# A smaller lead of the score maxima in an attention kernel, and the output projection's first pieces moved

## The reference, cut to what matters

```
# x: [2, 1024, 512], 32 heads of 16, all float32
x = x + layernorm(attention(layernorm(x)))          # stage A to C
x = x + layernorm(feed_forward(layernorm(x)))       # stage D: 512 -> 1376 -> 512, silu(gate) * up

# attention
q, k, v = split(x @ w_attn.T); q, k = rope(q), rope(k)
scores  = q @ k.T / sqrt(16), causal                # 1024 x 1024 for each of 64 heads
y       = softmax(scores) @ v
y       = y + gating * softmax(q @ ak.T / sqrt(512)) @ av      # 10 adapter rows
out     = y @ w_proj.T
```

## Time and profile before

| | before |
|---|---|
| three runs | 1182.92, 1190.9, 1196.09 us, median 1190.9 |
| the profiled execution | 1182.43 us, of which the span from first to last instruction is 1180.7 us |
| PE busy | 1095.5 us, 93% of the span |
| DVE, ACT, POOL busy | 703.0, 500.9, 255.1 us |
| mean granted clock of PE | 0.962 of full |
| attention | from about 230 us to 746 us of the span |

### The profile page before, as it was taken

The page is one execution under the profiler, slowest core; times in us unless marked ns, Lnnn a source line. Parts: engine busy times, 40 slices in busy tenths (PEclk is TensorE's granted clock), DMA queues, the critical chain, the costliest instruction groups (busy, mean ns, idle before and its releaser), DMA issues. The chain is left out here.

```text
span 1180.7 us, 18091 instructions
## 1 busy us (share of the span) xinstructions
PE 1095.5 (93%) x7020; PEld 750.4 (64%) x7020; DVE 703.0 (60%) x975; ACT 500.9 (42%) x1054; POOL 255.1 (22%) x255
## 2 busy tenths in 40 slices
PE   3999999888999999999999998889999999999996
PEld 1878778644454555555545444577887887887884
DVE  4748565776777778888888763583634324324113
ACT  3233242334776777777777655224321121121110
POOL 3517255400221111111111133451001001001001
PEclk9999999856999999999999998999999999999998
DMA  6265767733444444445444332645323003001000
GB/s 252 75 178 152 164 177 170 157 78 54 83 84 83 83 84 83 87 94 96 88 84 96 125 104 89 202 160 161 107 58 107 1 1 107 1 1 59 13 1 36
DMA packets 93869, 113.08 MB, mean 96 GB/s; under 512 B 26456, under 2 KB 54744, under 8 KB 93784
## 3 DMA queue, kind: packets, MB, share of 16 engines
q1 hardware_dynamic: 91720, 108.07, 35.9%
q10 hardware_dynamic: 2064, 3.85, 2.0%
HBM read 68.82 MB, written 42.21 MB: 94 GB/s over the span
## 5 line engine op out<-in xcount | busy, mean ns | idle before, releaser
L841 ACT ACTIVATE prob<-ps_s 128x512 f32<-128x512 f32 (+3 forms) x768 | 323.7, 497 | 173.9 <-PE ps_s L991 167.3
L865 DVE TENSOR_REDUCE neg<-ps_m 128x2 f32<-128x1024 f32 (+2 forms) x224 | 248.2, 1144 | 60.4 <-PE ps_m L956 38.3
L991 PE MATMUL ps_s<-q_op,k_op 50*128 50x512 f32 (+2 forms) x768 | 242.3, 448 | 18.4 <-ACT prob L841 13.5
L956 PE MATMUL ps_m<-k_op,q_op 48*128 48x512 f32 (+2 forms) x768 | 186.2, 422 | 9.9 <-DVE neg L865 7.1
L991 PEld LDWEIGHTS ps_s<-q_op,k_op 50*128 50x128 f32 x768 | 117.5, 192 | 120.2 <-ACT prob L841 61.8
L799 POOL TENSOR_SCALAR_AFFINE_SELECT prob<-prob 128x512 f32<-128x512 f32 x128 | 83.3, 651 | 396.7 <-ACT prob L841 396.6
L1005 PE MATMUL ps_y<-prob,vg 128*17 128x512 f32 (+3 forms) x1536 | 152.5, 517 | 0.0
L1577 DVE TENSOR_TENSOR hf<-sl,ps_u 128x512 f32<-128x512 f32 (+1 forms) x44 | 30.2, 686 | 171.5 <-PE ps_u L78 150.8
L865 DVE TENSOR_REDUCE neg_far<-ps_m 128x4 f32<-128x512 f32 (+2 forms) x96 | 100.2, 1048 | 31.1 <-PE ps_m L961 29.5
L956 PEld LDWEIGHTS ps_m<-k_op,q_op 48*128 48x128 f32 x768 | 97.4, 199 | 29.7 <-DVE neg L865 20.4
L1642 PE MATMUL ps_d<-w_high,wp_high 128*128 128x512 f32 (+1 forms) x352 | 115.2, 390 | 0.3 <-DVE wp_high L1579 0.3
(11 more groups left out here) (175 smaller groups left out, 1689.1 us busy)
## 6 DMA issues: line engine op xcount, KB each, us to landing
y_heads<-y_sb SPq DMA_DIRECT2D x32, 256.0 KB, 2.1
raw<-in_w_ffn SPq DMA_DIRECT2D x31, 256.0 KB, 3.3
k_op<-k_parts SPq DMA_DIRECT2D x28, 256.0 KB, 4.4
q_op<-q_parts SPq DMA_DIRECT2D x56, 128.0 KB, 5.0
v_groups<-v_out SPq DMA_DIRECT2D x16, 272.0 KB, 4.1
x<-in_x SPq DMA_DIRECT2D x4, 1024.0 KB, 7.8
q_parts<-part_h SPq DMA_DIRECT2D x16, 256.0 KB, 2.9
q_parts<-part_l SPq DMA_DIRECT2D x16, 256.0 KB, 2.9
```

The source lines that it names most:

```text
L841: act.activation(prob[:, v % NPROB, h, unit_cols(u)], ps_s[:, y % NS, unit_cols(u)], ACT.Exp, scale=D ** -0.5).then_inc(s_exp, 1)
L865: nc.vector.tensor_reduce(to[:, :, pairs[0]:pairs[-1] + 1, i - TT * c], scores, axis=AX.X, op=ALU.max, negate=True).then_inc(a_read, 1)
L956: last = nc.tensor.matmul(ps_m[:, g % 2, s, base:base + wide], q_op[buf][r, c, pair, (i - TT * c) * P:(i - TT * c + 1) * P], k_op[buf][r, ...
L991: nc.tensor.matmul(ps_s[:, y % NS, lo:BLK], k_op[buf][r, pair, j * P:(j + 1) * P], q_op[buf][r, c, pair, lo:BLK], start=True, stop=True)\
```

## The change

LEAD falls from 11 to 3. Group 0 now holds 36 M steps instead of 45 (eight chunks and one turn less), every later group still 22, but other chunks stand in the slots of the pattern, and the list of maxima runs out nine slots later, in the tenth unit of group 14. The slots of `beside` move with it: the four parts of the first projected piece now all stand in group 15, together with those of the second piece. What POOL, ACT and DVE do for these pieces moves to later places.

```
-LEAD = 11
+LEAD = 3
@@ POOL, behind the mask of unit u of group n
-                if (n, u) == (NG - 2, 3):
+                if (n, u) == (NG - 2, 10):
                     tail.add_adapter(pool, 0)
-                if (n, u) == (NG - 2, 9):
+                if (n, u) == (NG - 1, 1):
                     tail.add_adapter(pool, 1)
-                if (n, u) == (NG - 2, 11):
-                    tail.add_adapter(pool, 2)
-                if (n, u) == (NG - 1, 2):
+                if (n, u) == (NG - 1, 3):
                     tail.inverse_deviation(pool, 0)
                     tail.residual_pool(pool, 0)
-                if (n, u) == (NG - 1, 3):
+                    tail.add_adapter(pool, 2)
                     tail.inverse_deviation(pool, 1)
                     tail.residual_pool(pool, 1)
@@ ACT
-        highs = {(NG - 2, 9): 0, (NG - 2, 11): 1, (NG - 1, 2): 2, (NG - 1, 11): 3}
+        highs = {(NG - 1, 0): 0, (NG - 1, 3): 1, (NG - 1, 7): 2, (NG - 1, 11): 3}
@@ DVE, behind the last maxima
         weights(NG - 4, range(2))
+        tail.low(dve, 0)
         tail.divide(dve, 1)
         weights(NG - 4, range(2, 4))
-        tail.low(dve, 0)
+        tail.low(dve, 1)
+        weights(NG - 3, range(4, 5))
+        finish(0)
         tail.divide(dve, 2)
-        weights(NG - 3, range(4, 6))
-        tail.low(dve, 1)
-        finish(0)
+        weights(NG - 3, range(5, 6))
+        finish(1)
         tail.low(dve, 2)
-        finish(1)
         tail.divide(dve, 3)
@@ PE, which work stands in which slot behind the list of maxima
-        (tail.spread, 1, (5, 6)), (tail.spread, 2, (9, 10)),
-        (tail.project, 0, (11, 12, 14, 16)), (tail.project, 1, (19, 21, 23, 25)),
-        (tail.spread, 3, (28, 30))
+        (tail.spread, 1, (5, 6)), (tail.project, 0, (7, 8, 9, 10)),
+        (tail.spread, 2, (11, 12)), (tail.project, 1, (14, 15, 16, 17)),
+        (tail.spread, 3, (19, 20))
```

More of the change, by code:

```diff
@@ L1037, in _ @@
         beside = {}
-        for step, m, slots in ((first_spread, 0, (1, 2)), (last_turn, 0, (3,)), (tail.spread, 1, (5, 6)), (tail.spread, 2, (9, 10)),
-                               (tail.project, 0, (11, 12, 14, 16)), (tail.project, 1, (19, 21, 23, 25)),
-                               (tail.spread, 3, (28, 30))):
+        for step, m, slots in ((first_spread, 0, (1, 2)), (last_turn, 0, (3,)), (tail.spread, 1, (5, 6)),
+                               (tail.project, 0, (7, 8, 9, 10)), (tail.spread, 2, (11, 12)),
+                               (tail.project, 1, (14, 15, 16, 17)), (tail.spread, 3, (19, 20))):
             beside.update((slot, (step, m, part)) for part, slot in enumerate(slots))
```

## The result

The changed kernel takes 1242.7 us (median of 4 runs, 1236.4 to 1250.3) where the kernel before takes 1190.7: a ratio of 1.046, 95% interval 1.042 to 1.050. It is slower by 52 us, and the forecast of 1196 with its range up to 1212 was wrong. The profiled execution took 1243.97 us, its span is 1242.3 us, and its mean granted clock is 0.905 where it was 0.962.

The account below looks back on a forecast made before the run. It took PE and ACT to pace alternating stretches of each group, PE around the products and ACT among the scores. Terms -6 - 2.5 + 11.7 + 2 = +5.2 us on the median 1190.9 gave 1196 us, range 1183 to 1212.

Parts of the forecast that it names:

- Part 1, group 0: Group 0 of attention: nine M steps leave it, saving 6 us, plus 2.5 us from a clock dip that should go.
- the second term: Behind group 0's end: the half-clock dip from 289.4 to 296.2 should go, -2.5 us, from 0 to -3.4.
- Part 2, the steady groups: Groups 1 to 13: same work in other slots, 0.9 us longer each, +11.7 us in all, from +5 to +16.
- the wait: Group's end: PE waits 0.5 us ahead of turn 1 for DVE's read of k1, where it waited for nothing before.
- Part 3, the tail: End of attention: eight chunks and a turn come back in group 14, +2 us, from -1 to +6.
- The two waits: End of attention: first projection's wait for DVE's low and second's for normalize stay unchanged, 2.8 us in all.
- POOL's cover: End of attention: last products may wait for masks behind POOL's earlier work; one or two us, not in the sum.
- SP at no cost: SP's queue: stores and loads go out about 6 us later, maxima still land with 3 us of room; cost 0.
- Rival C: Steady groups: the new 0.5 us wait at the turn drops the clock in each group, +21 us, 1217 us; chance 0.09.
- against: a group would still be busy near 95%: Steady groups: the prediction's argument that PE, still busy near 95%, speaks against the clock falling in each group.

Follow-up runs that it names:

- no_masks: Kernel before, with the causal masks of chunks k14 and k15 left out in groups 1 to 14: 1215.0 us, ratio 1.021.
- single: Changed kernel with the products in twelve single blocks, one behind each second score pair, M steps where they were: 1191.2 us, ratio 1.003.
- far_late: Changed kernel with the second half's far-key chunks first and turn 1 moved from behind score pair 22 to behind 24: 1239.0 us, ratio 1.042.
- slots: Changed kernel with chunks reordered so each slot holds nearly its contents from before the change, turn 1 at the group's end: 1254.9 us, ratio 1.055.
- tail_only: Changed kernel with LEAD back at 11, the tail's steps kept at their changed places: 1185.6 us, ratio 0.999.
- slots2: slots with turn 0 three M slots earlier and POOL's second inverse deviation ahead of unit 10's mask: 1215.6 us, ratio 1.026.
- turn_late: Changed kernel with turn 1 moved from behind score pair 22 to behind pair 24: four executions from 1197.6 to 1270.1 us, no ratio given.
- far_first: Changed kernel with the second half's far-key chunks, which include masked ones, ahead of the near-key ones: 1237.0 us, ratio 1.040.
- split_a: Changed kernel with the double block of products behind score pair 2 split into single ones behind pairs 4 and 7: 1250.6 us, ratio 1.051.
- zone_twice: Changed kernel with the matmuls of chunks k6, k7 and k8 issued twice in groups 1 to 14: 1220.6 us, ratio 1.028.

## Why the prediction was wrong

**Part 1, group 0** (forecast -6 and -2.5): -8.4 us up to group 1's first copy of y. The sum is right, in part by luck. The dip that the second term wanted gone did not go: 6.8 us at half clock behind 289 in the earlier trace rows, now 3.4 at 283.1 and 3.4 at 293.3. Instead the long stretch at half clock ahead of it, which the prediction left as it was, ends at 272.9 and not at 279.1 and is 6.8 us shorter. How the 8.4 us divide between fewer steps and clock no run shows.

**Part 2, the steady groups** (forecast +0.9 us a group): right in what it priced, and the step that failed is what it left out. At full clock the group is 1.06 us longer, inside the forecast 0.4 to 1.2. PE's timeline at the end of a group, answering to the earlier trace rows:

```profile
448.27 0.39 PE L955 MATMUL ps_m<-k_op,q_op 48*128 48x256 f32 x2
...
448.89 0.36 PE L990 MATMUL ps_s<-q_op,k_op 50*128 50x256 f32 x2
449.09 0.34 PE L955 MATMUL ps_m<-k_op,q_op 48*128 48x384 f32 x2
...
449.37 0.80 PE L990 MATMUL ps_s<-q_op,k_op 50*128 50x256 f32 x2
450.41 0.28 PE L972 MATMUL ps_m<-ident,neg 128*16 128x128 f32 x1 [0.24 <-DVE neg L863]
450.61 0.50 PE L990 MATMUL ps_s<-q_op,k_op 50*128 50x256 f32 x3
```

From the end of the products at 448.27 to the next scores at 450.61 are 2.34 us, where it was 1.47 and was forecast at 2.3; the wait is 0.24 and not 0.5, since the score pair ahead of it is later by as much. What failed is the sentence that closes this part: "Cheap chunks now stand in slots paced by ACT, where they gain nothing". They lose there. With k6, k7, k8 and turn 0 where k14 to k17 stood PE streams nothing but scores, maskless chunks and a turn from pair 4 to pair 10, and the clock falls there in 12 of 13 groups. With what falls in b and d that makes 12.2 us at 1.2 GHz a group, 53 us in all. The slots of b changed in the same way: k19, k0, k1 and k2, all with masks, gave way to k10 to k13 without. Masks taken out of two of a's slots in the old kernel bring the fall there too (no_masks), and products put between the chunks end it (single). Both are shown by the runs. Not shown is that the contents alone decide: far_late and slots fall in a with masks there. The prediction read a wait of PE's weight loads for ACT as free room, and took the clock as given.

**Part 3, the tail** (+2, from -1 to +6): +2.7 in the profiled execution, and nothing in the median of tail_only. The two waits did not stay; PE's timeline there, answering to the earlier trace rows:

```profile
769.89 0.50 PE L1307 MATMUL ps_o<-wp_high,y_h 128*128 128x512 f32 x1 [0.43 <-DVE y_l L1190]
...
804.89 2.35 PE L1004 MATMUL ps_y<-prob,vg 128*17 128x512 f32 x32
```

The first projection waits 0.43 us where it waited 1.84, the second for nothing, and the last products start without a wait, so POOL's cover held. SP at no cost: right, from group 1 on no wait of PE for the maxima appears in the changed kernel (group 0 has two, 2.3 and 0.3 us, and had 2.0 and 0.3 before); what a late landing costs is seen in slots.

**Rival C** (0.09, 1217 us) came nearest, for a wrong reason. It had the clock fall in each group but by the new wait, at 1.6 us a group; it is 4.1. Its "against: a group would still be busy near 95%" is the error in the weighing: PE was busy 95% ahead of the fall at 460.60 and throughout ahead of the one at 498.15, and 11 of single's 13 groups, busy 95%, do not fall. The Trainium skill, page "TensorE: Matmul & The Clock Gate", section "A second HAM failure mode: psum-queue depth-cycling", blames short idle times between groups of matmuls. Ahead of the changed kernel's falls in a there is no idle time of over 0.06 us, and no_masks falls with the waits of the kernel before, so here that is not needed. In slots2 11 of 12 falls stand at a wait of 0.6 us, which all 13 groups have; that agrees with the page, though the chunks ahead of that wait have no masks either, and no run parts the two.

What stays open: what makes d weak in turn_late, far_first and split_a, where it holds masks, while the kernel before passes d without masks in 11 of 13 groups; why a falls in far_late and slots; why one and the same stretch is passed at full clock in some groups and not in others, and why turn_late's executions differ by 72 us; and whether a full clock goes with a short lead and the group of 28.4 us. No version with a shorter lead beat the kernel before; single comes nearest (1.003).

## What to carry to other kernels

When steps are moved between slots of a kernel whose clock is full, look at what each stretch of PE's stream is left with, also where another engine sets the pace: small matmuls in seemingly free room (here 16 masks a group, 0.10 us for four) can be what keeps the clock up, and their loss cost 29 us. PE's busy share did not warn of it here. The kinds of matmuls in the stretch did for stretch a, but not for every fall in every version, so a new order has to be measured. Repeating a matmul in a suspected stretch, with the falls counted by place, tests the suspicion.

## What the runs showed of the hardware that was not expected

- The granted clock fell to 1.2 GHz behind a stretch in which PE's records are busy throughout (498.15), and stayed at 2.4 GHz in groups that are busy 94.8% (single). Just ahead of 11 of the changed kernel's 12 falls in stretch a stood scores (50 rows), chunks (48 rows) and one turn, without products or masks; ahead of the twelfth stood four product matmuls too.
- Work added made the kernel faster: 6 matmuls more a group, some 20 us less (zone_twice against the changed kernel). Work removed made it slower: 16 fewer, 29 us more (no_masks).
- A microsecond at half clock costs 0.38 us here, not 0.5: 60.2 us (443.4 less 13 x 29.48) for 158.8 us at 1.2 GHz. That it is under half fits a group in which PE waits for ACT and DVE in part anyway; no run shows this reason.
- One program's executions can differ by 6%, with the granted clock going along (turn_late, 1197.6 to 1270.1 us at 0.951 to 0.882).
